# Phase one's rows as two fp16 parts in three slots, two units side by side

## The reference

```
h = relu(layernorm(x))
xs = [h[src,:8], h[dst,:8]]                      # 16 scalars an edge
xv = [h[src,8:], h[dst,8:]] as 16 vectors of 3
hid = sqrt(2) * relu(attr10 @ W1 / sqrt(10))     # 16
w = (hid @ W2 / 4) as (E, 7, 16, 8)              # a weight matrix for each edge
s_out, g_out, v_out = sums over u of xs, xv, xv.unit, ... times w
msg = [tanh(s_out), tanh(g_out) * v_out] * norm
x = x + segment_sum(msg, dst)
```

## Time and profile before

| | |
|---|---|
| median of three runs | 1189.8 us (1189.35 to 1199.52) |
| span of the profiled execution | 1442.6 us |
| busy: PE, DVE, ACT, POOL | 856.9, 982.3, 842.4, 794.9 us |
| share of the span | 59%, 68%, 58%, 55% |
| chain that ended last | PE 21%, ACT 21%, DVE 20%, unknown queue 16%, DVEq 10% |
| mean granted TensorE clock | 0.760 |

### The profile page before, as it was taken

How to read it: one execution, slowest core, us unless ns; L and a number is a source line. 1 busy time by engine, 2 the same in 40 slices (tenths; PEclk the granted TensorE clock), 3 DMA queues, 4 the chain that set the end, 5 groups by cost and what they waited for, 6 DMA issues and landing times.

```text
span 1442.6 us, 16871 instructions
## 1 busy us (share of the span) xinstructions
PE 856.9 (59%) x5248; PEld 690.5 (48%) x5248; DVE 982.3 (68%) x1799; ACT 842.4 (58%) x2035; POOL 794.9 (55%) x796
## 2 busy tenths in 40 slices
PE   0256777677776877777874221323135777777773
PEld 0245665566565756666773110211123565555552
DVE  4566686777776667566664635865336999998984
ACT  0346665666766575666754333746244887787871
POOL 5664565466554665455004455775752665656664
PEclk9988688878777777767786555555557999999986
DMA  4121021111111102111014213432300000000000
GB/s 114 19 56 35 16 50 22 43 28 46 58 41 29 37 10 62 34 36 23 16 52 163 76 37 84 115 109 76 88 20 5 10 9 9 9 9 9 9 9 7
DMA packets 40669, 60.52 MB, mean 42 GB/s; under 512 B 17361, under 2 KB 31077, under 8 KB 40324
## 3 DMA queue, kind: packets, MB, share of 16 engines
q1 hardware_dynamic: 12216, 46.86, 10.2%
q0 software_dynamic: 25184, 12.32, 5.4%
q10 hardware_dynamic: 3180, 0.26, 0.2%
HBM read 40.33 MB, written 19.37 MB: 41 GB/s over the span
## 4 chain that ended last, share of the span: by engine, by line
PE 21%; ACT 21%; DVE 20%; another core or an unknown queue 16%; DVEq 10%; issue 8%; SPq 1%; DMA 1%; POOL 0%; POOLq 0%
PE sums L1080 9%; ACT h1d_or_products L809 5%; DVEq L1764 4%; PE tens L1070 3%; ACT below L900 3%; PE turnB L1056 3%; PE turnA L1056 2%; ACT stack_turned L800 2%; DVEq L1705 2%; DVE run L1753 2%; ACT agg_or_stacks L800 2%; DVE tens L1725 2%; PE tens L1074 2%; DVE dcen L1748 1%
## 5 line engine op out<-in xcount | busy, mean ns | idle before, releaser
L674 POOL DMA_INDIRECT x_rows<-in_x,src_index x196 | 196.1, 1001 | 228.9 <-PE tens L1074 146.3
L701 POOL DMA_INDIRECT out_dram<-agg_or_stacks,scatter_index x196 | 193.6, 988 | 144.6 <-ACT agg_or_stacks L974 90.4
L694 POOL DMA_INDIRECT agg_or_stacks<-run_sums,sum_row_index x196 | 203.1, 1036 | 112.3 <-issue 57.9
L674 POOL DMA_INDIRECT x_rows<-in_x,dst_index x196 | 197.2, 1006 | 64.9 <-issue 64.9
L1408 DVE TENSOR_TENSOR h1d_or_products<-tens,hid 128x768 f32<-128x768 f32 x168 | 158.8, 952 | 64.8 <-PE tens L1074 42.8
L1080 PE MATMUL sums<-h1d_or_products,ident 128*128 128x192 f32 x896 | 174.4, 356 | 4.8 <-issue 4.2
L1080 PEld LDWEIGHTS sums<-h1d_or_products,ident 128*128 128x128 f32 x896 | 164.9, 212 | 11.3 <-issue 11.1
L1143 PE MATMUL sums<-one_column,halves_or_steps 128*128 128x1 f16 x112 | 22.1, 197 | 176.6 <-DVE halves_or_steps L1564 62.0
L967 ACT ACTIVATE features_or_rows<-stack_turned,is_last 128x132 f32<-128x132 f32 x196 | 85.9, 520 | 39.3 <-DVE stack_turned L1735 39.3
L1143 PEld LDWEIGHTS sums<-one_column,halves_or_steps 128*128 128x128 f16 x112 | 14.1, 126 | 197.7 <-ACT below L900 73.2
L1070 PE MATMUL tens<-w_scalar_stacks,agg_or_stacks 96*128 96x384 bf16 x196 | 66.5, 432 | 65.9 <-ACT h1d_or_products L809 41.4
(11 more groups left out here) (308 smaller groups left out, 2536.5 us busy)
## 6 DMA issues: line engine op xcount, KB each, us to landing
src_everywhere<-src_by_columns SPq DMA_DIRECT2D x14, 896.0 KB
xin<-in_x SPq DMA_DIRECT2D x27, 449.5 KB
out_dram<-xin SPq DMA_DIRECT2D x27, 449.5 KB
x_rows<-in_x,src_index POOLq DMA_INDIRECT x196
x_rows<-in_x,dst_index POOLq DMA_INDIRECT x196
run<-run_sums SPq DMA_DIRECT2D x1, 3136.0 KB
agg_or_stacks<-run_sums,sum_row_index POOLq DMA_INDIRECT x196
out_dram<-agg_or_stacks,scatter_index POOLq DMA_INDIRECT x196
```

The lines of the kernel that those rows point to most:

```text
L674: nc.gpsimd.indirect_dma_start(xs[:, t, side, :], None, x, bass.IndirectOffsetOnAxis(ap=idx[:, t:t + 1], axis=0)).then_inc(s_gath[g % LEAD ...
L694: nc.gpsimd.indirect_dma_start(aggr[:, t, :], None, rs, bass.IndirectOffsetOnAxis(ap=ridx[:, t:t + 1], axis=0)).then_inc(s_rsg[t // GA], 16)
L701: nc.gpsimd.indirect_dma_start(out, bass.IndirectOffsetOnAxis(ap=sidx[:, t:t + 1], axis=0), aggr[:, t, :], None, bounds_check=N - 1, oob_i ...
```

## The change

The normalised rows are scaled by 4096 (through the variance's square root) and W2 by a factor found on chip, so that its largest element becomes 16384; the hidden values take both factors out again. With that, two fp16 parts of a row and three products of parts stand in for three bf16 parts and six: three slots of 16 channels, 48 partitions a unit. Two units lie side by side in the 96 partitions of one transpose: units 0 (scalars) and 1 (product with the direction) in the first, two vector components in the second, the third component and the first unit of the next tile in the last, of which the product reads the lower 48 partitions. A tile has 3 transposes (`TURNS = 3`) and 3 matmuls of 384, 256 and 128 columns. The 21 transposes of a group are three chunks of 7, all of them turned in the group before.

```
-    SLOTS = 6
+    SLOTS = 3
     UNITS = 5
-    KU = SLOTS * VU
+    KU = 2 * SLOTS * VU
+    TURNS = 3
-    NCH = UNITS * GA // CH
+    NCH = TURNS * GA // CH
...
             sp.wait_ge(s_w2p, 1)
-            for place, which in enumerate((0, 0, 1, 1, 2, 0)):
-                rows = slice(place * VU, (place + 1) * VU)
+            for place, which in enumerate((0, 1, 0)):
                 for u in range(2):
-                    sp.dma_start(w_s[rows, u, :, :], w2s_part[u * VU:(u + 1) * VU, which]).then_inc(s_w2, 16)
-                sp.dma_start(w_v[rows, :, :], w2v_part[:, which]).then_inc(s_w2, 16)
+                    rows = slice((u * SLOTS + place) * VU, (u * SLOTS + place + 1) * VU)
+                    sp.dma_start(w_s[rows, :, :], w2s_part[u * VU:(u + 1) * VU, which]).then_inc(s_w2, 16)
+                    sp.dma_start(w_v[rows, :, u * MOUT:(u + 1) * MOUT], w2v_part[:, which]).then_inc(s_w2, 16)
...
             def first_parts(n):
                 act.wait_ge(s_h, n + 1)
-                nc.scalar.copy(stack[:, :, 0:SLOTS:2, :], spread(hflat, 2, [P, UNITS * GA, 3, VU])).then_inc(s_hi, 1)
-
-            def second_parts(n):
-                act.wait_ge(s_r1, n + 1)
-                nc.scalar.copy(stack[:, :, 1:4:2, :], spread(rest, 2, [P, UNITS * GA, 2, VU])).then_inc(s_mid, 1)
+                nc.scalar.copy(slots[:, :, 0:2, :], spread(hflat, 2, [P, UNITS * GA, 2, VU])).then_inc(s_hi, 1)
...
                 if next1:
+                    take_emb(g + 1)
                     first_parts(g + 1)
-                    take_emb(g + 1)
-                    second_parts(g + 1)
...
-                if next1:
-                    turned(g + 1, 1 - b, range(2, 3))
                 if past(g, 0):
                     keep_run(g - 1, 1 - b)
-                if next1:
-                    turned(g + 1, 1 - b, range(3, 4))
                 flags(g, b)
                 if next1:
-                    turned(g + 1, 1 - b, range(4, NCH))
+                    turned(g + 1, 1 - b, range(2, NCH))
...
                     for i in range(CH):
-                        mm = nc.tensor.transpose(bank[:, i * P:(i + 1) * P],
-                                                 stack[:, c * CH + i].rearrange("p s c -> p (s c)"), identb[:])
+                        t, u = divmod(c * CH + i, TURNS)
+                        at = (t * UNITS + 2 * u) * SLOTS * VU
+                        mm = nc.tensor.transpose(bank[:, i * P:(i + 1) * P], stack[:, at:at + KU], identh[:])
                     mm.then_inc(s_turn, 1)
...
                 bank = tens[(b + t) % 2]
-                for i, u in enumerate((0, UNITS - 1)):
-                    nc.tensor.matmul(bank[:, 0:HID * OG], stackT[b][:, UNITS * t + u, :],
-                                     w_s[:, i].rearrange("c j o -> c (j o)"), start=(i == 0), stop=(i == 1))
+                nc.tensor.matmul(bank[:, 0:HID * OG], stackT[b][:, TURNS * t, :], w_s[:].rearrange("c j o -> c (j o)"),
+                                 start=True, stop=True)
                 vec = bank[:, 512:512 + HID * OG].rearrange("p (j o) -> p j o", o=OG)
-                for k in range(3):
-                    mm = nc.tensor.matmul(vec[:, :, k * MOUT:(k + 1) * MOUT], stackT[b][:, UNITS * t + 1 + k, :], w_v[:],
-                                          start=True, stop=True)
-                mm.then_inc(s_tens, 1)
+                nc.tensor.matmul(vec[:, :, 0:2 * MOUT], stackT[b][:, TURNS * t + 1, :], w_v[:], start=True, stop=True)
+                nc.tensor.matmul(vec[:, :, 2 * MOUT:], stackT[b][0:KU // 2, TURNS * t + 2, :],
+                                 w_v[0:KU // 2, :, 0:MOUT], start=True, stop=True).then_inc(s_tens, 1)
...
                 if more:
                     turn_emb(g + 1)
-                turn_units(g, b, range(2, 4))
                 if past(g, 0):
                     sum_first(g - 1)
-                turn_units(g, b, range(4, NCH))
                 product(g, b, 2)
                 if past(g, 0):
                     sum_rest(g - 1)
                 product(g, b, 3)
                 if more:
                     hidden_product(g + 1)
+                    turn_units(g + 1, 1 - b, range(1))
                 product(g, b, 4)
+                if more:
+                    turn_units(g + 1, 1 - b, range(1, 2))
                 product(g, b, 5)
                 if more:
-                    turn_units(g + 1, 1 - b, range(2))
+                    turn_units(g + 1, 1 - b, range(2, NCH))
                 product(g, b, 6)
...
-            def first_rest(n):
+            def second_part(n):
                 dve.wait_ge(s_hi, n + 1)
-                v.tensor_tensor(rest, hflat, stack[:, :, 0, :], ALU.subtract).then_inc(s_r1, 1)
-
-            def third_part(n):
-                dve.wait_ge(s_mid, n + 1)
-                v.tensor_tensor(stack[:, :, SLOTS - 1, :], rest, stack[:, :, 1, :], ALU.subtract).then_inc(s_lo, 1)
+                v.tensor_tensor(slots[:, :, 2, :], hflat, slots[:, :, 0, :], ALU.subtract).then_inc(s_lo, 1)
```

More of the change, by code:

```diff
@@ L21 @@
 TANH_GAIN = 1.593
+ROW_GAIN = 4096.0
+W2_TOP = 16384.0
 PW_S = 0.17677669529663687
@@ L43, in build_gnn @@
     NR = 2 * GA
-    SLOTS = 6
+    SLOTS = 3
     UNITS = 5
-    KU = SLOTS * VU
-    TACT = 3
-    NDV = GA - 1
+    KU = 2 * SLOTS * VU
+    TURNS = 3
+    BY_ACT = (3,)
+    BY_DVE = tuple(t for t in range(GA) if t not in BY_ACT)
+    NDV = len(BY_DVE)
+    NACT = len(BY_ACT)
+    FIRST = 3
     CH = 7
-    NCH = UNITS * GA // CH
+    NCH = TURNS * GA // CH
     DP = 124
@@ L162, in build_gnn @@
         hrow = part(agg, at, GA, UNITS, VU)
-        at += NR * ROW
-        rest = part(agg, at, UNITS * GA, VU)
         at += NR * ROW
@@ L237, in build_gnn @@
         assert at <= T * FEAT
-        numer = part(turned_area[:, :, :].rearrange("p u e -> p (u e)").bitcast(F32), 0, 2, HEADS * F1, GA + 1)
+        numer = part(turned_area, 0, 2, HEADS * F1, GA + 1)
         late = sb("halves_or_steps", [P, CT * P // 2 + 4 * T])
-        first_half = part(late, 0, 2 * TACT, HID // 2, OG)
+        first_half = part(late, 0, 2 * FIRST, HID // 2, OG)
         vb = sb("src_everywhere", [P, CT * P])
@@ L854, in group @@
                     gates(g - 1)
-                multiply(g, b)
+                multiply(g, b, BY_ACT[0])
                 if next2:
@@ L1029, in _ @@
             mm.then_inc(s_gps, 1)
+            pe.wait_ge(s_wmax, 1)
+            nc.tensor.transpose(small[0:1, 3 * P:3 * P + SC], wmax[:, 0:1], ident[0:SC, 0:SC]).then_inc(s_wmaxT, 1)
+            pe.wait_ge(s_wtop, 1)
+            nc.tensor.matmul(small[:, 3 * P + SC:3 * P + SC + 1], ones_row[:], wtop[:], start=True, stop=True
+                             ).then_inc(s_wall, 1)
             pe.wait_ge(s_flags, 1)
@@ L1120, in _ @@
             hidden_product(0)
-            turn_units(0, 0, range(2))
+            turn_units(0, 0, range(NCH))
             group(0, 0)
@@ L1251, in _ @@
             v.memset(dprev_i, 0).then_inc(s_padf, 1)
+            v.memset(stack[:, GA * UNITS * SLOTS * VU:], 0.0)
+            v.memset(w_v[:], 0.0)
             v.memset(w1bd[:], 0.0)
@@ L1345, in _ @@
             v.drain()
-            for which in range(3):
-                for whole, left, parts in ((w2s, w2s_rest, w2s_part), (w2v, w2v_rest, w2v_part)):
-                    v.tensor_copy(parts[:, which], whole if which == 0 else left)
-                v.drain()
-                for whole, left, parts in ((w2s, w2s_rest, w2s_part), (w2v, w2v_rest, w2v_part)):
-                    if which < 2:
-                        v.tensor_tensor(left, whole if which == 0 else left, parts[:, which], ALU.subtract)
-                v.drain()
+            v.memset(wmax[:, 2:4], 0.0)
+            v.tensor_reduce(wmax[:, 0:1], w2s.rearrange("p j o -> p (j o)"), AX, ALU.max)
+            v.tensor_reduce(wmax[:, 1:2], w2s.rearrange("p j o -> p (j o)"), AX, ALU.min)
+            v.drain()
+            v.tensor_reduce(wmax[0:VU, 2:3], w2v.rearrange("p j o -> p (j o)"), AX, ALU.max)
+            v.tensor_reduce(wmax[0:VU, 3:4], w2v.rearrange("p j o -> p (j o)"), AX, ALU.min)
+            v.drain()
+            v.scalar_tensor_tensor(wmax[:, 0:2], wmax[:, 1::2], -1.0, wmax[:, 0::2], ALU.mult, ALU.max)
+            v.drain()
+            v.tensor_tensor(wmax[:, 0:1], wmax[:, 0:1], wmax[:, 1:2], ALU.max)
+            v.drain().then_inc(s_wmax, 1)
+            dve.wait_ge(s_wmaxT, 1)
+            v.tensor_reduce(wtop[:], small[0:1, 3 * P:3 * P + SC], AX, ALU.max)
+            v.drain().then_inc(s_wtop, 1)
+            dve.wait_ge(s_wall, 1)
+            v.tensor_scalar(hid_gain[:], small[:, 3 * P + SC:3 * P + SC + 1], 1e-30, 1.0 / W2_TOP, ALU.max, ALU.mult)
+            v.drain()
+            v.reciprocal(wgain[:], hid_gain[0:SC])
+            v.drain()
+            v.tensor_scalar(hid_gain[:], hid_gain[:], 2.0 ** 0.5 / (4 * EMB ** 0.5 * ROW_GAIN), None, ALU.mult)
+            v.tensor_scalar(w2s, w2s, wgain[:, 0:1], None, ALU.mult)
```

(7 more changed lines are left out.)

120 lines of the change are left out of this document (66 added, 54 removed).

## The result

The changed kernel takes **1213.57 us** (median of 4 runs, 1210.9 to 1214.03); on the same chip the kernel before takes 1189.57 (1186.81 to 1199.52). The ratio is 1.018, with an interval of 1.0131 to 1.0226. The forecast was 1171, in a range of 1135 to 1205: it is slower, and outside the range.

What follows compares the result with a forecast made beforehand. A phase-one chain through TensorE, largely at half clock, was taken to bind; 11 x -1.5, 10 x -0.5 and 6 x 0.5 gave -18.5 us, set-up -1, total about -19 from 1189.8: 1171 us, range 1135 to 1205.

Steps and rivals of the forecast that it cites:

- the model of a timed group: Late phase-one group of the profile before, free of unexplained waits, taken to stand for timed groups: 20.8 us.
- 28 groups of 20.8 us are 582: Check on phase one: 101 us less than the stretch's 683.5, called a fair share of the 237 us unknown queue.
- halved sums at half clock: TensorE's 16 sums of halved tiles: nearly all at half clock after the change, 3.7 us against 2.73.
- The saving of 2.2 us ahead of them: TensorE's transposes and products before the halved sums: fewer columns and sets, work ending at 9.7 after the sums' end.
- T2's wait: Third set of transposes, between products 5 and 6, waits for ScalarE's copy: starts at 6.2 us plain, 7.2 dense.
- The half-clock work behind it: TensorE's chain after that wait: transposes 0.75, product 6 0.65, product 1 0.80, emb turn 0.21, halved sums 3.7 us.
- VectorE ready at 21.6 in dense-dense groups: Where two dense groups follow each other VectorE sets the step, 21.6 instead of 21.1: +0.5 us in 6 steps.
- ScalarE over 3 us less busy per group, and 0 in the sum: ScalarE's casts and copies in phase one: 3.4 us off per group, none of it on the chain.
- Set-up -1: Before phase one: SyncE's stack loads -3.8 us, VectorE's longer preparation 3, so -1 in all, range -3 to +5.
- Rival one: Phase one, clock comes back later because TensorE pauses twice: 1225 at worst, 1205 more likely; chance 0.15.
- Rival two: Phase one, TensorE's clock rises sooner or does not fall: 1134 or 1150, range 1125 to 1155; chance 0.18.
- the signs given for being wrong: Profile after: clock share moves by over 0.05, the third transposes do not wait, or dense-slice groups take over 22 us.

Runs made afterwards that it cites:

- r2_before: The kernel before, unchanged, profiled beside the changed kernel on one chip of the faster kind: 1191.81 us, profile span 1188.0.
- r2_after: The changed kernel, unedited, profiled on the same chip as the kernel before: 1213.04 us, 1.0179 of before, profile span 1210.7.
- T2 late: Changed kernel with the third set of transposes moved from between products 5 and 6 to behind the next emb turn: 0.9972 of before (faster chips), 0.943 (slower).
- both filled: Changed kernel plus 32 unread matmuls a group before the hidden product and 12 behind product 5: 1175.75 us, 0.9874 of before, on the faster chips.
- the fill: Changed kernel plus 32 unread matmuls a group ahead of the hidden product: 1337.6 us, 0.9532 of before, on the slower chips.
- copy first: Changed kernel with ScalarE copying the turned sets ahead of the squares: 1331.96 us, 0.9497 of before; repeats 0.9423, 0.9397, 0.9486, all on the slower chips.

## Why the prediction was wrong

**The step that failed** is "I therefore take the group from 699.98 us as the model of a timed group". The gap of 252.8 us between span and median was seen, and put down to the late signals alone. But the group without them was of a chip B as well: there the plain model group takes 20.8 us with nine of TensorE's 11.15 us at half clock. On A the 11 full steps of before that start from a plain group take 19.1 on the mean, (9 x 19.47 + 2 x 17.6) / 11; the dense ones are near the model (20.3 and 20.7). The check "28 groups of 20.8 us are 582" was compared with an uncertain remainder and could not catch that: 27 steps are 562 us by the model and 538.4 on A. So 23 of the 37 us between forecast (-18.5 in phase one) and result (+18.9) are a baseline that was taken too slow.

What this did to the saving shows in the plain steps of r2_before and r2_after, by their timelines, all counted from the sums' end:

| | work ahead of the halved sums ends | halved sums take | step |
|---|---|---|---|
| model group, B | 11.9 | 2.7 | 20.8 |
| before on A, mean of 11 | 10.4 | 2.6 | 19.1 |
| forecast for after | 9.7 | 3.7 | 19.3 |
| after on A, mean of 11 | 10.4 | 3.8 | 20.15 |

The cost of the change, halved sums at half clock, was forecast (1.0 us) and came. The saving of 2.2 us ahead of them did not: it was taken from a stretch of 10.2 us at half clock, and on A that stretch is shorter (6.8 us in 12 of the 22 dips of the clock in phase one of before) or absent, as in four of the 11 plain steps, which take 17.6. There is less for fewer columns to save, and T2's wait takes the place of what is saved. The clock of after was forecast near 0.77 and is 0.76; what the profile from B could not show is that before stands at 0.84 on A.

The other 14 us (543 forecast for phase one after, 557.3 measured) are terms of the new chain, each sized a little too small: 20.15 for the 11 steps that start plain (19.3 forecast), 20.6 for dense to plain (20.3), 21.6 for dense to dense (21.3), which is 9 + 3 + 2. The parts, one by one:

- *T2's wait* was sized right: start of T2 at 6.2 (plain) and 7.2 (dense) after the sums' end; in r2_after it is 6.27 (298.68 to 304.95) and 7.15 (318.73 to 325.88). Only in the second of two dense groups is it later, 7.7 to 8.3.
- *The half-clock work behind it* was not: in the plain step from 298.68 T2 takes 0.95 us (0.75 forecast), product 6 0.76 (0.65), product 1 0.90 (0.80), the emb turn 0.36 (0.21), the halved sums 3.83 (3.7), product 2 0.43 (0.35) and the sums 5.41 (5.27). Part of this is the clock, which came back at about 312.7, 14.0 us after the sums' end and not 13.3.
- *Halved sums*: over all 28 groups they go from 2.76 to 3.86 us on the mean, 31 us in all, more than the whole loss.
- *VectorE ready at 21.6 in dense-dense groups*: measured 21.63. Its +0.5 was counted from 21.1 for before; on A that is 20.74, so +0.9.
- *ScalarE over 3 us less busy per group, and 0 in the sum*: 421.8 to 332.3 is 3.3 a group, and it bought nothing on A.
- *Set-up -1*: +0.9 on A, -0.8 on B (77.0 to 76.2 us, two chips). On A the chain of the first 70 us is GpSimd's gathers (57% before, 73% after), not the loads of the earlier trace rows; there shortening the loads could not help.
- The 2.9 us behind phase one lie in code that is not changed. T2 late and both filled have 586.9 and 582.7 us there, so it moves by some us from profile to profile; its cause was not looked for.

Rival one named the right places (a clock that comes back later, and T2's wait), was given 0.15 and priced at +35 at the worst and +15 as likelier; the result was +24. Its worst price was added up wrongly: 9.7 + 3.8 + 0.65 + 7.0 is 21.2, not 21.5, which makes +27. And the sums did not slow down as it assumed (5.41 us, not 7.0). Rival two's condition, a clock that stays up, did not come by itself but by the filling. By the rule that the prediction took from the Trainium skill ("TensorE: Matmul & The Clock Gate", Part 4: PE-mode transpose) alone, two sets of transposes fewer should not lower the clock; it fell, from 0.84 to 0.76. But the columns of the products fell by a third in the same change, so this does not speak against the rule, and no run here took the transposes away by themselves. Nor do and the earlier trace rows, as the prediction says: products 5, 6, 0 and 1 ran from 709.62 on, ahead of the transposes that it counts. Of the signs given for being wrong one held, and only with before measured on A: there the clock share moved by 0.08, against the bound of 0.05. T2 did wait, and the dense groups took under 22 us.

What stays open: why results of TensorE reach others up to 8 us late on chips B (the DMA packets take as long there as on A: 10.2% of 1442.6 us and 12.6% of 1188.0 for the largest queue); where most of the gain on B comes from; why the clock fell on A, which the thinner work is only a likely reason for; whether T2 late and the fill add up on A; whether copy first would do there what T2 late does; and whether the kernel before would gain by a fill on A as well.

## What to carry to other kernels

Where the profiled span and the timed median are far apart, none of the profile's stretches can stand for the timed run, the quiet ones neither: take a second profile, or give the whole sum a second value, by a shorter baseline group. After matmuls are taken out of a cycle with pauses, look at the granted clock of the stretch that stays on the chain: here it went down and the change cost more than it saved, and matmuls that nobody reads, put in the pauses, turned a loss of 1.8% into a gain of 1.3%. And an operation moved ahead in TensorE's queue needs its release from another engine at that moment, or all the products queued behind it wait with it. A mean over the steps of a pipeline should leave out the last one, in which it runs empty.

## What the runs showed of the hardware

- Chips of two kinds (or in two conditions): the kernel before at 1190 and at 1404 to 1419 us, the same code, with up to 8 us between the end of transposes and the start of the copy that waits for them on the latter; the same change made the kernel 1.8% slower on one and 5.5% faster on the other.
- Some 1150 unread 128x128 matmuls (3660 instructions against 2504 in phase one) made phase one 41 us shorter on A, with a granted clock of 0.90 instead of 0.76. On B, 48 of them a group raised the clock of the kernel before to 0.885 and did not make it faster (1.0053 and 1.0136).
- In the changed kernel the clock went through phase one in stretches of about 10.2 us at full and at half rate, nearly in step with groups of 20.1 to 21.6 us.
